# Where a graph-attention kernel gets its neighbour channels from: all from HBM, or half of them copied on the chip

## The chip, the core and the metric

The kernel runs on one core of a Trainium2 chip. The metric is the device time of one execution in microseconds (us). A core has the engines TensorE (PE in the profile; its weight loads PEld), VectorE (DVE), ScalarE (ACT), GpSimd (POOL) and SyncE (SP), and 16 DMA engines that move data between the memory of the chip (HBM) and the on-chip memory SBUF, or inside SBUF. The compute engines reach SBUF by partition (128 of them), and PSUM holds what TensorE writes.

## The reference

x has 16 images of 256 channels and 64 x 32 positions, fp32. All that is computed of an image:

```python
alpha = bn_relu(einsum('bchw,oc->bohw', x, wa), ...)      # 32 channels
sigma = bn_relu(einsum('bchw,oc->bohw', x, ws), ...)      # 32 channels
att = einsum('bkn,bkm->bnm', alpha, sigma)
att = softmax(where(adj, att, NEG), axis=2)               # adj: the 8 spatial neighbours
h_s = einsum('bnm,bcm->bcn', att, x)
Gc = einsum('bcn,bdn->bcd', x, x)
catt = softmax(where(cadj, Gc, NEG), axis=2)              # cadj: channels c-1 and c+1 alone
h_p = einsum('bcd,bdn->bcn', catt, x)
out = (1 - gama) * x + gama * elu(h_s + h_p)
```

What matters for the change is h_p: channel c of the output gets channel c-1 and channel c+1 of x, each times a weight of its own.

## The kernel before

**Tiles.** Partition p holds the channels 2p (h = 0) and 2p + 1 (h = 1). Three buffers xs hold images of x, 128 x 2 x 2048 elements with a row of zeros ahead and behind. `upper` (two buffers) holds x once more, by position instead of by channel, in halves of 1024 and 1152 KB. An image is worked on in four quarters of 512 positions (QUARTERS, QN = 512), so there are 64 steps; step s is quarter s mod 4 of image s // 4.

**The neighbour channels.** For h = 0 the neighbours of channel 2p are 2p + 1, which is in the same partition of xs, and 2p - 1, which is in partition p - 1. For h = 1 they are 2p, in the same partition, and 2p + 2, in partition p + 1. The neighbour in the same partition is handled by ACT (`weigh_own`, L301), which writes weight times x (plus 1) into PSUM tile z. The other neighbour lies in another partition, where an engine can't reach it, and so the host lays out a third copy of x (`x_near`) in which it stands in the right partition: h = 0 gets channel 2p - 1, h = 1 gets channel 2p + 2, zeros at the ends. It is loaded into `near` (two buffers) one quarter at a time, 128 x 2 x 512 elements, 512 KB (`load_near`, L173). `mix_channels` on DVE (L383) multiplies it by its weight and adds it to z. Then TensorE adds the spatial part to z (`z_sums`), from `upper` and the transposed probabilities.

**The rest of a step.** TensorE computes the scores, DVE masks them and takes maxima, ACT the exponentials, DVE normalises, TensorE transposes, ACT moves the result to SBUF, TensorE runs the two phases of `z_sums`, ACT and DVE take the ELU (`exp_z`, `elu_out`), and POOL scales and adds x (`keep_x` L237, `add_elu` L243 and L247) into `blend`, which SP stores. Once an image TensorE projects x of the next image onto queries and keys (`project_odd` in the step of quarter 0, `project_query`, `project_even`) and computes the products of neighbouring channels from `upper` (`gram_band`, in the step of quarter 3), from which DVE and ACT make the channel weights catt.

**Order.** Each engine runs a list of instructions written out in the order of the steps t, with waits on semaphores. All big DMAs are issued by SP, on one queue. In step t = 4b + q, SP waits for the scores and transposes, loads a quarter of near of image b + 1, waits for the first phase of z_sums of the step before (`z_half`), loads a half of x of image b + 2 (q = 0 and 2), the second half of upper of image b + 1 (q = 1) or the first half of upper of image b + 2 (q = 3), and stores the result of step t - 2. A half of upper is loaded only once `z_done` tells that the image two before has been used up; so the second half, issued in the step of q = 1, is wanted by `gram_band` two steps later. Ahead of the loop stand the loads of the first images: x(0), upper(0), the constants, then, behind a wait for `project_odd(0)`, the first quarter of near(0) and both halves of x(1), and behind the first scores the other three quarters of near(0).

Of the kernel before, what the change touches and what calls it, by code (L numbers as in the profile page):

```python
# [6 lines left out]
B, C, H, W = 16, 256, 64, 32  # L7
HID = C // 8
P = 128
HALF = C // P  # L10
N = H * W
QUARTERS = P // HID
QR = H // QUARTERS
QN = QR * W
# [5 lines left out]
XBUFS = 3  # L20
# [6 lines left out]
SIDES, PAIRS, POWERS = 100, 104, 108  # L27
EVEN, ODD = 5 * KEYS, 4 * KEYS
HALVES = N // 2


C_ID, C_DOWN = 0, P
# [8 lines left out]
def graph_attention(nc, x, x_t, x_near, w_t, vectors, constants, out):  # L41
# [15 lines left out]
    with ctx:  # L57
        def sb(name, shape, dt=fp32):
            return ctx.enter_context(nc.sbuf_tensor(name, shape, dt))
# [4 lines left out]
        def sem(name):  # L64
            return ctx.enter_context(nc.semaphore(name))

        xs = [sb(f"x{j}", [P, HALF, N + 4 * W]) for j in range(XBUFS)]
        near = [sb(f"near{j}", [P, QUARTERS, HALF, QN]) for j in range(2)]
        upper = [sb(f"upper{j}", [P, GROUPS + 1, C]) for j in range(2)]
        const = sb("const", [P, C_ALL])  # L70
        zeros_b = sb("zeros_b", [P, QN], bf16)
# [18 lines left out]
        catt = sb("catt", [P, 2, 2])  # L90
# [15 lines left out]
        masks_in = sem("masks_in")  # L106
        ident_in = sem("ident_in")
        x_in = [[sem(f"x_in{j}{i}") for i in range(2)] for j in range(XBUFS)]
        near_in = [[sem(f"near_in{j}{q}") for q in range(QUARTERS)] for j in range(2)]
        upper_in = [[sem(f"upper_in{j}{i}") for i in range(2)] for j in range(2)]  # L110
        stored = [sem(f"stored{i}") for i in range(BLENDS)]
        pads_done = sem("pads_done")
        zeros_done = sem("zeros_done")
        bn_step = sem("bn_step")
        bn_var = sem("bn_var")
# [24 lines left out]
        mix_done = sem("mix_done")  # L140
# [12 lines left out]
        def real(s):  # L153
            return 0 <= s < STEPS

        def cols(q):
            return slice(W + q * QN, W + (q + 1) * QN)

        @block.sync
        def _(sp):  # L160
            def load_x(b, i):
                if b >= XBUFS:
                    s = (b - XBUFS) * QUARTERS + 2 * i + 1
                    sp.wait_ge(even_done, b - XBUFS + 1)
                    sp.wait_ge(product_done, 2 * s + 2)
                    sp.wait_ge(keep_done, s + 1)
                sp.dma_start(xs[b % XBUFS][:, :, W + i * HALVES:W + (i + 1) * HALVES],
                             x_img[b][:, :, i * HALVES:(i + 1) * HALVES]).then_inc(x_in[b % XBUFS][i], 16)

            def load_near(b, q):  # L170
                if b >= 2:
                    sp.wait_ge(mix_done, 2 * ((b - 2) * QUARTERS + q) + 2)
                sp.dma_start(near[b % 2][:, q, :, :], x_near[b, q]).then_inc(near_in[b % 2][q], 16)  # L173

            def load_by_key(b, i):
                if b >= 2:
                    sp.wait_ge(z_done, (b - 2) * QUARTERS + 2 * i + 2)
                part = slice(i * GROUPS // 2, (i + 1) * GROUPS // 2 + i)
                sp.dma_start(upper[b % 2][:, part, :], x_t[b][:, part, :]).then_inc(upper_in[b % 2][i], 16)

            def store(s):
                b, q = s // QUARTERS, s % QUARTERS
                if s < TAIL:
                    sp.wait_ge(blend_done, s + 1)
                    sp.dma_start(out_img[b, :, :, q * QN:(q + 1) * QN], blend[s % BLENDS][:, :, :])\
                        .then_inc(stored[s % BLENDS], 16)
                else:
                    for h in range(HALF):
                        sp.wait_ge(tail_done, 2 * (s - TAIL) + h + 1)
                        sp.dma_start(out_img[b, :, h, q * QN:(q + 1) * QN], blend[s % BLENDS][:, h, :])\  # L190
                            .then_inc(stored[s % BLENDS], 16)

            sp.dma_start(const[:, 0:C_BAND], constants[:, 0:C_BAND]).then_inc(ident_in, 16)
            load_x(0, 0)
            load_x(0, 1)
            load_by_key(0, 0)
            load_by_key(0, 1)
            sp.dma_start(const[:, C_BAND:], constants[:, C_BAND:]).then_inc(masks_in, 16)
            sp.wait_ge(odd_done, 1)
            load_near(0, 0)  # L200
            load_x(1, 0)
            load_x(1, 1)
            sp.wait_ge(score_done, 2)
            for q in range(1, QUARTERS):
                load_near(0, q)
            load_by_key(1, 0)
            for t in range(STEPS + 2):
                b, q = t // QUARTERS, t % QUARTERS
                if real(t):
                    sp.wait_ge(score_done, t - t % 2 + 2)  # L210
                    if t > 0:
                        sp.wait_ge(pt_done, t)
                if b + 1 < B:
                    load_near(b + 1, q)
                if t > 0 and real(t):
                    sp.wait_ge(z_half, t)
                if q % 2 == 0 and b + 2 < B:
                    load_x(b + 2, q // 2)
                if q == 1 and b + 1 < B:
                    load_by_key(b + 1, 1)  # L220
                if q == 3 and b + 2 < B:
                    load_by_key(b + 2, 0)
                if real(t - 2):
                    store(t - 2)
            for i in range(BLENDS):
                sp.wait_ge(stored[i], 16 * (STEPS // BLENDS + (i >= TAIL % BLENDS)))

        @block.gpsimd
        def _(pool):
            def keep_x(s):  # L230
                b, q = s // QUARTERS, s % QUARTERS
                if s == 0:
                    pool.wait_ge(bn_var, 1)
                pool.wait_ge(x_in[b % XBUFS][q // 2], 16 * (b // XBUFS + 1))
                if s >= BLENDS:
                    pool.wait_ge(stored[s % BLENDS], 16 * (s // BLENDS))
                nc.gpsimd.tensor_scalar(blend[s % BLENDS][:, :, :], xs[b % XBUFS][:, :, cols(q)], mix[:, 0:1],  # L237
                                        0.0 if s < TAIL else mix[:, 1:2],
                                        ALU.mult, ALU.add).then_inc(keep_done, 1)

            def add_elu(s):
                pool.wait_ge(elu_done, 2 * s + 2)
                nc.gpsimd.tensor_scalar(elu[s % 2][:, :, :], elu[s % 2][:, :, :], vec[:, V_GAMA:V_GAMA + 1], mix[:, 1:2],  # L243
                                        ALU.mult, ALU.add).then_inc(gama_done, 1)
                pool.wait_ge(keep_done, s + 1)
                pool.wait_ge(gama_done, s + 1)
                nc.gpsimd.tensor_tensor(blend[s % BLENDS][:, :, :], elu[s % 2][:, :, :], blend[s % BLENDS][:, :, :],  # L247
                                        ALU.add).then_inc(blend_done, 1)

            for j in range(XBUFS):  # L250
                nc.gpsimd.memset(xs[j][:, :, 0:W], 0.0).then_inc(pads_done, 1)
                nc.gpsimd.memset(xs[j][:, :, W + N:N + 2 * W], 0.0).then_inc(pads_done, 1)
            pool.wait_ge(bn_done, 1)
            for t in range(STEPS + 2):
                if real(t - 1):
                    keep_x(t - 1)
                if 0 <= t - 2 < TAIL:
                    add_elu(t - 2)
# [84 lines left out]
        def _(dve):  # L343
# [33 lines left out]

            def mix_channels(s, h):
                b, q = s // QUARTERS, s % QUARTERS
                dve.wait_ge(near_in[b % 2][q], 16 * (b // 2 + 1))  # L380
                dve.wait_ge(product_done, 2 * s + h + 1)
                zh = z[s % 2][h]
                nc.vector.scalar_tensor_tensor(zh[:, :], near[b % 2][:, q, h, :], catt[:, h, h:h + 1],  # L383
                                               zh[:, :], ALU.mult, ALU.add).then_inc(mix_done, 1)

            def elu_out(s, h):
# [40 lines left out]
            part = vec[:, 0:8].rearrange("p (s n) -> p n s", s=2)  # L427
# [15 lines left out]
            for t in range(STEPS + 2):  # L443
                b, q = t // QUARTERS, t % QUARTERS
# [215 lines left out]
```

## Time and profile before

| | |
|---|---|
| Median of 3 runs (lowest, highest) | 419.72 us (418.23, 424.91) |
| The profiled execution | 416.75 us, span 415.0 us |
| Mean granted clock of TensorE | 0.964 of full speed |
| PE busy | 364.1 us, 88% of the span |
| PEld busy | 277.5 us, 67% |
| DVE busy | 315.5 us, 76% |
| ACT busy | 305.8 us, 74% |
| POOL busy | 291.6 us, 70% |
| DMA | 137.74 MB in 40613 packets, mean 332 GB/s |
| The chain that ended last, by engine | PE 32%, DMA 30%, DVE 20%, ACT 9%, issue 7% |
| Issues: x | 32 of 1024 KB, 9.1 us from issue to landing |
| Issues: near | 64 of 512 KB, 7.8 us |
| Issues: upper | 16 of 1152 KB, 8.4 us, and 16 of 1024 KB, 7.9 us |
| Issues: stores | 62 of 512 KB, 8.0 us, and 4 of 256 KB, 2.1 us |

The profiled execution is one run of the program with the profiler on; its time of 416.75 us is the span of the core's work and 1.75 us around it. Busy is the sum of the times in which an engine ran an instruction. The chain follows what released what, back from the last instruction. "Issue" is time in which nothing that the profile shows was waited for. The time to landing is from the issue of a DMA by SP until its semaphore is full, so it holds the time that it stood in the queue behind others.

### The profile page before, as it was taken

The page shows a single profiled execution, that of the slowest core. Times are in us where ns is not written, and L with a number is a line of the kernel's source. Part 1 is how long each engine was busy: PE and PEld are TensorE (multiplying, and loading weights), DVE is VectorE, ACT ScalarE, POOL GpSimd, SP SyncE. Part 2 cuts the span into 40 slices and gives each one's busy share as a digit, 9 for nine tenths or more (in the row PEclk, how much of TensorE's full clock was granted, in tenths as well). Part 3 has the DMA queues.
Part 4 walks back from the last instruction along what each step waited for, and adds up shares of the span by engine and source line. Part 5 has one row for each costly group of instructions (what it writes and reads, how often), then busy time and mean ns, then how long its engine had stood idle before and what let it go on. Part 6 is the DMA issues. An engine that isn't in the chain of part 4 may idle for free.

```text
span 415.0 us, 14346 instructions
## 1 busy us (share of the span) xinstructions
PE 364.1 (88%) x5487; PEld 277.5 (67%) x5488; DVE 315.5 (76%) x1072; ACT 305.8 (74%) x900; POOL 291.6 (70%) x198
## 2 busy tenths in 40 slices
PE   5977998989998999999899999999989898999783
PEld 1546767666766867676686767677676667767662
DVE  1166978778787688879768887978788697888775
ACT  2178686868878497887849788787869678686761
POOL 2007686787868588787858878788868858787861
PEclk9889999999999899999989999999999899999778
DMA  8999999999999899999999999999999999985213
GB/s 274 414 368 404 315 344 357 366 359 347 364 346 385 292 358 366 388 364 351 356 317 337 382 385 360 363 378 383 342 367 358 365 307 367 341 297 202 103 53 152
DMA packets 40613, 137.74 MB, mean 332 GB/s; under 512 B 3296, under 2 KB 3552, under 8 KB 36448
## 3 DMA queue, kind: packets, MB, share of 16 engines
q1 hardware_dynamic: 40256, 136.76, 91.4%
q8 instruction: 43, 0.70, 0.6%
q14 instruction: 26, 0.21, 0.1%
q10 hardware_dynamic: 288, 0.07, 0.1%
HBM read 103.26 MB, written 33.55 MB: 330 GB/s over the span
## 4 chain that ended last, share of the span: by engine, by line
PE 32%; DMA 30%; DVE 20%; ACT 9%; issue 7%; SPq 0%; DVEq 0%; ACTq 0%
DMA upper<-x_t_dram 28%; PE gb L468 17%; PE z L468 11%; ACT score L281 6%; DVE probs L374 5%; DVE elu L389 5%; PE tr L543 3%; DVE z L383 3%; ACT z L301 3%; DMA x<-x_dram 2%; DVE gb L404 1%; DVE band L400 1%; DVE row_inv L370 1%; DVE pair_inv L420 1%; DVE catt L421 1%
## 5 line engine op out<-in xcount | busy, mean ns | idle before, releaser
L468 PEld LDWEIGHTS z<-probs_t,upper 64*128 64x128 f32 x2304 | 155.6, 191 | 44.6 <-issue 28.8
L468 PE MATMUL z<-probs_t,upper 64*128 64x128 f32 (+1 forms) x2304 | 173.5, 284 | 5.1 <-ACT probs_t L292 2.4
L247 POOL TENSOR_TENSOR blend<-elu,blend 128x1024 f32<-128x1024 f32 x62 | 146.2, 2358 | 9.5 <-POOL elu L243 0.4
L243 POOL TENSOR_SCALAR elu<-elu,vec,mix 128x1024 f32<-128x1024 f32 x62 | 74.0, 1193 | 98.5 <-DVE elu L389 98.5
L308 ACT ACTIVATE elu<-z 128x512 f32<-128x512 f32 x128 | 69.6, 597 | 60.6 <-PE z L468 60.6
L389 DVE SCALAR_TENSOR_TENSOR elu<-elu,z 128x512 f32<-128x512 f32 x124 | 79.5, 683 | 28.7 <-ACT elu L308 28.3
L301 ACT ACTIVATE z<-x,catt 128x512 f32<-128x512 f32 x128 | 83.6, 693 | 14.2 <-DVE catt L421 14.1
L281 ACT ACTIVATE score<-score,neg_max 128x128 f32<-128x128 f32 x256 | 86.2, 337 | 7.4 <-DVE neg_max L365 7.3
L383 DVE SCALAR_TENSOR_TENSOR z<-near,catt,z 128x512 f32<-128x512 f32 x128 | 90.3, 751 | 1.5 <-ACT z L301 1.5
L237 POOL TENSOR_SCALAR blend<-x,mix 128x1024 f32<-128x1024 f32 x64 | 72.0, 1126 | 6.5 <-DMA x<-x_dram 6.5
L468 PE MATMUL gb<-x,wt 128*32 128x256 f32 (+2 forms) x720 | 65.1, 480 | 2.5 <-DMA x<-x_dram 2.5
L365 DVE CUSTOM_DVE_ANT_0 score<-score,const 128x128 f32<-128x128 f32 x256 | 66.4, 322 | 1.1 <-PE score L468 1.1
L543 PE MATMUL tr<-const,probs 128*128 128x128 f32 x256 | 42.9, 291 | 17.0 <-DVE probs L374 16.4
L468 PE MATMUL gb<-upper 128*64 128x65 f32 (+1 forms) x1088 | 41.5, 237 | 14.9 <-DMA upper<-x_t_dram 14.8
L281 ACT ACTIVATION_READ_ACCUMULATOR score<-score,neg_max 128x1 f32 x256 | 51.9, 203 | 0.0
L468 PEld LDWEIGHTS gb<-upper 128*64 128x64 f32 (+1 forms) x1088 | 38.4, 149 | 19.8 <-issue 18.5
L374 DVE TENSOR_TENSOR probs<-score,row_inv 128x512 f32<-128x512 f32 x64 | 44.3, 692 | 2.4 <-DVE row_inv L370 0.3
L543 PEld LDWEIGHTS tr<-const,probs 128*128 128x128 f32 x256 | 27.4, 143 | 24.5 <-DVE probs L374 23.2
L292 ACT ACTIVATE probs_t<-tr 128x512 f32<-128x512 f32 x64 | 38.4, 600 | 5.8 <-PE tr L543 5.7
L468 PE MATMUL score<-key,query 32*64 32x128 f32 x1024 | 36.5, 279 | 0.0
L365 DVE DVE_READ_ACCUMULATOR2_ANT neg_max<- 128x1 f32 x256 | 36.3, 142 | 0.0
L468 PEld LDWEIGHTS gb<-x,wt 128*32 128x32 f32 x720 | 19.0, 110 | 23.6 <-issue 14.9
(49 smaller groups left out, 145.0 us busy)
## 6 DMA issues: line engine op xcount, KB each, us to landing
x<-x_dram SPq DMA_DIRECT2D x32, 1024.0 KB, 9.1
near<-x_near_dram SPq DMA_DIRECT2D x64, 512.0 KB, 7.8
out_dram<-blend SPq DMA_DIRECT2D x62, 512.0 KB, 8.0
upper<-x_t_dram SPq DMA_DIRECT2D x16, 1152.0 KB, 8.4
upper<-x_t_dram SPq DMA_DIRECT2D x16, 1024.0 KB, 7.9
out_dram<-blend SPq DMA_DIRECT2D x4, 256.0 KB, 2.1
const<-constants_dram SPq DMA_DIRECT2D x1, 291.5 KB, 12.0
const<-constants_dram SPq DMA_DIRECT2D x1, 128.0 KB, 2.2
```

Of the source, the lines that this page charges most:

```text
L237: nc.gpsimd.tensor_scalar(blend[s % BLENDS][:, :, :], xs[b % XBUFS][:, :, cols(q)], mix[:, 0:1], 0.0 if s < TAIL else mix[:, 1:2], ALU.mul ...
L243: nc.gpsimd.tensor_scalar(elu[s % 2][:, :, :], elu[s % 2][:, :, :], vec[:, V_GAMA:V_GAMA + 1], mix[:, 1:2], ALU.mult, ALU.add).then_inc(ga ...
L247: nc.gpsimd.tensor_tensor(blend[s % BLENDS][:, :, :], elu[s % 2][:, :, :], blend[s % BLENDS][:, :, :], ALU.add).then_inc(blend_done, 1)
L281: last = nc.scalar.activation(at, at, ACT.Exp, bias=neg_max[s % 2][:, v:v + 1], scale=-1.0, accum_out=row_sum[s % 2][:, v:v + 1])
L301: nc.scalar.activation(z[s % 2][h][:, :], xs[b % XBUFS][:, 1 - h, cols(q)], ACT.Identity, scale=catt[:, h, 1 - h:2 - h], bias=1.0).then_in ...
L308: nc.scalar.activation(elu[s % 2][:, h, :], z[s % 2][h][:, :], ACT.Exp, bias=-1.0)\
L365: last = nc.vector.tensor_tensor_reduce(at, at, mask, -1.0, TOP, ALU.add, ALU.min, neg_max[s % 2][:, v:v + 1])
L374: nc.vector.tensor_tensor(probs[s % 2][:, :, :], score[s % 2][:, :].rearrange("p (v m) -> p v m", m=WIN), row_inv[s % 2][:, :].unsqueeze(2 ...
L383: nc.vector.scalar_tensor_tensor(zh[:, :], near[b % 2][:, q, h, :], catt[:, h, h:h + 1], zh[:, :], ALU.mult, ALU.add).then_inc(mix_done, 1)
L389: nc.vector.scalar_tensor_tensor(to, elu[s % 2][:, h, :], 1.0, z[s % 2][h][:, :], ALU.min, ALU.max).then_inc(elu_done, 1)
L468: return nc.tensor.matmul(o, l, r, start=start, stop=stop, skip_group_check=True, **kw)
L543: last = nc.tensor.transpose(tr[:, v * P:(v + 1) * P], probs[s % 2][:, v, :], ident)
```

## The change

The h = 1 half of near, channel 2p + 2, is channel 2(p + 1), which is the h = 0 row of partition p + 1 of xs. It no longer comes from HBM: DMAs copy it inside SBUF from partitions 1 to 127 of xs into partitions 0 to 126 of near, in two pieces, 112 partitions and then 15. The h = 0 half still comes from HBM. near is loaded by halves of an image (1024 positions) instead of quarters: a DMA of 512 KB from HBM, a copy of 448 KB and one of 60 KB, whose three increments of 16 are awaited together (NEARS). Partition 127 of near's h = 1 half has no neighbour and must be zero; POOL sets both buffers of near to zero once, at the start. load_near has a wait more, for the half of x that it copies from, and at first for the zeros; load_x has a wait more, since a buffer of x may be overwritten only once it has been copied from. The steps in which near is loaded are now those of q = 0 and 2. The layout of x_near on the host shrinks to the h = 0 rows.

```diff
+SPREAD = 112
+NEARS = 3 * 16
...
-        near = [sb(f"near{j}", [P, QUARTERS, HALF, QN]) for j in range(2)]
+        near = [sb(f"near{j}", [P, HALF, N]) for j in range(2)]
...
-        near_in = [[sem(f"near_in{j}{q}") for q in range(QUARTERS)] for j in range(2)]
+        near_in = [[sem(f"near_in{j}{i}") for i in range(2)] for j in range(2)]
...
             def load_x(b, i):
...
+                    sp.wait_ge(near_in[(b - XBUFS) % 2][i], NEARS * ((b - XBUFS) // 2 + 1))
...
-            def load_near(b, q):
+            def load_near(b, i):
+                sp.wait_ge(x_in[b % XBUFS][i], 16 * (b // XBUFS + 1))
+                if b < 2:
+                    sp.wait_ge(near_zero, b + 1)
                 if b >= 2:
-                    sp.wait_ge(mix_done, 2 * ((b - 2) * QUARTERS + q) + 2)
-                sp.dma_start(near[b % 2][:, q, :, :], x_near[b, q]).then_inc(near_in[b % 2][q], 16)
+                    sp.wait_ge(mix_done, 2 * ((b - 2) * QUARTERS + 2 * i + 1) + 2)
+                j, signal, xb = b % 2, near_in[b % 2][i], xs[b % XBUFS]
+                part = slice(i * HALVES, (i + 1) * HALVES)
+                from_x = slice(W + i * HALVES, W + (i + 1) * HALVES)
+                sp.dma_start(near[j][:, 0, part], x_near[b][:, part]).then_inc(signal, 16)
+                for lo, hi in ((0, SPREAD), (SPREAD, P - 1)):
+                    sp.dma_start(near[j][lo:hi, 1, part], xb[lo + 1:hi + 1, 0, from_x]).then_inc(signal, 16)
...
             sp.wait_ge(score_done, 2)
-            for q in range(1, QUARTERS):
-                load_near(0, q)
+            load_near(0, 1)
             load_by_key(1, 0)
...
-                if b + 1 < B:
-                    load_near(b + 1, q)
+                if q % 2 == 0 and b + 1 < B:
+                    load_near(b + 1, q // 2)
...
                 nc.gpsimd.memset(xs[j][:, :, W + N:N + 2 * W], 0.0).then_inc(pads_done, 1)
+            for j in range(2):
+                nc.gpsimd.memset(near[j][:, :, :], 0.0).then_inc(near_zero, 1)
...
             def mix_channels(s, h):
                 b, q = s // QUARTERS, s % QUARTERS
-                dve.wait_ge(near_in[b % 2][q], 16 * (b // 2 + 1))
+                dve.wait_ge(near_in[b % 2][q // 2], NEARS * (b // 2 + 1))
                 dve.wait_ge(product_done, 2 * s + h + 1)
                 zh = z[s % 2][h]
-                nc.vector.scalar_tensor_tensor(zh[:, :], near[b % 2][:, q, h, :], catt[:, h, h:h + 1],
+                nc.vector.scalar_tensor_tensor(zh[:, :], near[b % 2][:, h, q * QN:(q + 1) * QN], catt[:, h, h:h + 1],
                                                zh[:, :], ALU.mult, ALU.add).then_inc(mix_done, 1)
```

## Rows read from the trace of the kernel before

**Rows 1.** The page: the span in 40 slices, the busiest DMA queue, and HBM traffic.

```profile
DMA  8999999999999899999999999999999999985213
GB/s 274 414 368 404 315 344 357 366 359 347 364 346 385 292 358 366 388 364 351 356 317 337 382 385 360 363 378 383 342 367 358 365 307 367 341 297 202 103 53 152
...
q1 hardware_dynamic: 40256, 136.76, 91.4%
...
HBM read 103.26 MB, written 33.55 MB: 330 GB/s over the span
```

**Rows 2.** Windows by stage: busy us of each engine (instructions), TensorE clock, DMA share, GB/s.

```profile
98.00:124.00 26.00, 23.59 (x360) 17.65 (x360) 21.39 (x70) 21.13 (x61) 20.29 (x14) 1.00 1.02 357
124.00:150.00 26.00, 23.23 (x350) 18.06 (x346) 19.86 (x70) 18.95 (x57) 18.75 (x13) 0.93 0.94 338
150.00:176.00 26.00, 24.72 (x386) 18.76 (x380) 22.14 (x77) 21.96 (x67) 21.64 (x14) 1.00 1.02 376
...
358.00:384.00 26.00, 24.20 (x398) 18.91 (x398) 21.97 (x80) 20.69 (x59) 20.06 (x14) 1.00 0.76 264
```

**Rows 3.** Waits of the engines: engine, line, releaser, us in total, times, longest us.

```profile
PE gb L468 <- DMA upper<-x_t_dram: 14.8, 14, 2.2
...
PE gb L468 <- DMA x<-x_dram: 2.5, 1, 2.5
```

**Rows 4.** Chain that ended last, in order of time: start us, us, what.

```profile
29.54 9.60 DMA upper<-x_t_dram
...
102.78 8.23 DMA upper<-x_t_dram
111.14 2.37 PE gb L468 x68
...
126.38 9.08 DMA upper<-x_t_dram
135.60 3.63 PE gb L468 x68
...
366.96 7.97 DMA upper<-x_t_dram
```

**Rows 5.** Windows near the start, where only loads move; columns as in the second group.

```profile
8.00:10.00 2.00, 0.00 (x0) 0.00 (x0) 0.00 (x0) 0.00 (x0) 2.00 (x2) 0.99 1.04 430
10.00:12.00 2.00, 1.81 (x20) 1.03 (x24) 0.00 (x0) 0.00 (x0) 0.00 (x0) 0.50 1.04 442
```

**Rows 6.** Windows at the end, where only stores move; columns as in the second group.

```profile
386.00:390.00 4.00, 2.75 (x27) 2.32 (x28) 3.93 (x13) 3.29 (x12) 3.29 (x4) 0.85 0.36 135
...
406.00:410.00 4.00, 2.65 (x36) 2.37 (x36) 1.97 (x4) 1.20 (x3) 0.62 (x1) 1.00 0.68 262
```

**Rows 7.** Instructions on tile near: count, ns min/median/max, first and last start us.

```profile
L383 DVE SCALAR_TENSOR_TENSOR z<-near,catt,z x128: 748/751/756, 21.8 to 402.9; 128x512 f32<-128x512 f32 x128
L173 SPq DMA_DIRECT2D near<-x_near_dram x64: 327/333/1103, 12.2 to 374.8; - x64
...
DMA to landing us min/median/max: 5.0/7.8/10.4
```

**Rows 8.** Landing of the loads of x: us from issue, min/median/max.

```profile
DMA to landing us min/median/max: 6.4/9.1/11.7
```

**Rows 9.** Timeline of TensorE near the start: start us, us, instruction, idle before it.

```profile
22.99 1.40 PE L468 MATMUL gb<-x,wt 128*32 128x256 f32 x16 [2.51 <-DMA x<-x_dram]
```

**Rows 10.** Timeline of GpSimd near the start, columns as in the group before.

```profile
1.14 0.15 POOL L252 MEMSET x<- 128x64 f32 x1
7.78 2.21 POOL L237 TENSOR_SCALAR blend<-x,mix 128x1024 f32<-128x1024 f32 x2 [6.49 <-DMA x<-x_dram]
32.95 1.19 POOL L243 TENSOR_SCALAR elu<-elu,vec,mix 128x1024 f32<-128x1024 f32 x1 [22.96 <-DVE elu L389]
```

**Rows 11.** Timeline of SP's DMA issues near the start, columns as before.

```profile
12.18 0.33 SPq L173 DMA_DIRECT2D near<-x_near_dram  x1
12.55 1.21 SPq L167 DMA_DIRECT2D x<-x_dram  x2
```

More of the change, by code:

```diff
@@ L112, in graph_attention @@
         pads_done = sem("pads_done")
+        near_zero = sem("near_zero")
         zeros_done = sem("zeros_done")
@@ L645 @@
     keys = keys.reshape(B, P, HALF, GROUPS + 1, WIN).transpose(0, 4, 3, 2, 1).reshape(B, WIN, GROUPS + 1, C)
-    beside = np.pad(a["x"].reshape(B, C, N), ((0, 0), (1, 1), (0, 0)))
-    beside = np.stack([beside[:, 0:C:2], beside[:, 3:C + 2:2]], axis=2)
-    beside = beside.reshape(B, P, HALF, QUARTERS, QN).transpose(0, 3, 1, 2, 4)
+    beside = np.pad(a["x"].reshape(B, C, N), ((0, 0), (1, 1), (0, 0)))[:, 0:C:2]
     arrays = {"x_dram": a["x"], "x_t_dram": keys, "x_near_dram": beside, "w_dram": w_t, "vectors_dram": vectors,
```

## The prediction, made before the change was run

> **What bounds the kernel now.** I read the page first. In its 40 slices the DMA line stands at 9 from the second slice to the thirty-fifth, and one queue, SP's, fills 91.4% of the 16 DMA engines' span with 136.76 MB [rows 1]. Is it really full where the work repeats? The windows say yes: share 0.94 to 1.02 at 338 to 376 GB/s, with TensorE busy 23 to 25 of 26 us, and only behind 358 us does the share fall, to 0.76 [rows 2]. Two resources are nearly full, so I looked for who waits for whom. TensorE waits for the upper tile (x by position) 14 times, 14.8 us in all, about 1 us an image, and once, 2.5 us, for x [rows 3]. The chain in order of time shows the loop: the load of an upper half is issued, lands 8 to 9.6 us later, gram_band starts at once, and 15 us of compute later the next one can be issued. From the piece at 29.54 to that at 366.96 there are 14 images: 24.1 us each [rows 4]. Those 8 us are mostly a place in a full queue: one MiB at the best rate of [rows 5], 430 GB/s, would take 2.4 us. So the DMA engines and TensorE's order are tied, DMA slightly the later: DMA time added to an image shows nearly whole, DMA time taken away shows only up to the 14.8 us of waits.
>
> How full is full? Loads alone ran at 430 and 442 GB/s [rows 5], stores alone at 135/0.36 = 375 and 262/0.68 = 385 GB/s per full share [rows 6]. HBM read is 103.26 MB and written 33.55 [rows 1], per image 6.45 and 2.10 MB. Unmixed that is 6.45/0.430 + 2.10/0.380 = 15.0 + 5.5 = 20.5 us. An image takes 24.1 at a share of about 0.99 [rows 2, 4], so 23.9. The 3.4 us between are lost when traffic out of SBUF mixes with loads: 3.4/2.10 = 1.6 us per MB going out.
>
> **Part by part.** A half image of near needs 1 MiB in both versions. Before, all came from HBM, in two DMAs of 512 KiB (64 in all). Now 512 KiB come from HBM in one DMA, 448 KiB are copied from 112 partitions of x and 60 KiB from 15: 96 issues instead of 64.
>
> Issues: 32 more at 0.33 us [rows 7] are 10.6 us of SP over the whole run, and SP spends its time in waits. I put them at nothing; if SP became late, their price would be 0.66 us an image.
>
> The load half. Same bytes, rows of 4 KB as before, issued up to one step earlier than the odd quarters were. It is read a whole image later, and a near load took at most 10.4 us [rows 7]: nothing. Ahead of the upper half in the queue stands the same number of bytes, issued about a step sooner.
>
> The copies, where all hangs. The trace of before has no transfer inside SBUF. Low end: a copy moves like loads alone, 0.524 MB/0.430 = 1.22 us, where in the steady mix at 357 GB/s [rows 2] a load costs 1.47: a gain of 0.25 us per half image. It could also relieve HBM: 1.04 of an image's 8.55 MB leave it, 12%, and 12% of the 3.4 us is 0.4 an image, 0.2 per half. High end: the 112 partitions at half rate, 0.459/0.215 = 2.13 us, and the 15 at a quarter, 0.061/0.108 = 0.57, together 2.70, a loss of 1.5 over the 1.22. What I take: a copy reads SBUF as a store does and writes it as a load does, so the nearest row is the mixing cost. 0.52 MB x 1.6 = +0.85 us per half, less 0.2 of relief: +0.65. Of the 32 halves the first two lie in the start and the last two where the share is 0.76 or falling; 28 x 0.65 = +18.2 us.
>
> The rows show that an on-chip row must pass the same 16 engines. The Trainium skill (DMA: Bandwidth & Descriptors, "Where 436 GB/s comes from") has it that the HBM side, about 358 GB/s, binds loads and the fabric, 435, binds copies inside SBUF; by that the copies would gain the 0.25 us per half and no more would be lost. This trace speaks against the first half of it: 430 and 442 GB/s of loads [rows 5].
>
> The start. The first half of near is issued at 12.18 us, right ahead of both halves of x(1) [rows 11]. It now carries 0.52 MB more, 1.2 us. TensorE waited 2.51 us for that very x until 22.99 us [rows 9]: +1.2 us on the path. mix_channels first runs at 21.8 us [rows 7], some 9.6 us behind the issue; hidden by about 4 us.
>
> The two memsets of near on GpSimd: 4096 elements a partition. A 64-column memset takes 0.15 us, a 1024-column operation 1.1 [rows 10]; so 4.5 us (by the second) to 9.7 us (64 x 0.152) each. Behind 1.3 us the first ends at 11 us at worst, before the issue at 12.18; the second by 20.7, before SP's first step. Both delay keep_x from 7.78 by up to 13 us, whose result add_elu takes at 32.95 [rows 10]: covered. Were it not, the start would slip by the excess.
>
> New waits on SP. load_near now waits for its half of x, issued one image (24 us) earlier and landed after at most 11.7 us [rows 8]; behind it in SP's order are the wait for z_half, the load of x, the store and the upper half. load_x waits for the near copy of three images back. Both long met: nothing. mix_channels waits for a half where it waited for a quarter: nothing, since near comes an image early.
>
> DVE reads 512 elements in a row as before: 751 ns stay [rows 7]. Less for nobody: no instruction of an engine goes.
>
> Sum: 416.75 (the profiled execution, whose span is 415.0) + 18.2 + 1.2 = 436.2, 4.7% over. The median of the runs is 419.72, 3 us above that execution, so I say 437.
>
> **The rivals.** Copies cost what loads cost. For it: row size and byte count are equal. Each half is 0 to 0.25 us dearer: 416.75 + 1.2 + 0 to 7 = 418 to 425; no difference that a measurement of this kernel can tell, which starts at 2%, 8.4 us.
>
> Relief decides, and the time falls. The mechanism: reads from HBM are what stalls, and with 16% fewer of them the queue drains sooner, so the upper half lands before TensorE asks. 0.25 + 0.2 per half x 28 = 12.6 us, less 1.2: 405. It is capped by the 14.8 us of waits [rows 3], plus what the clock gives back: gram_band took 2.37 us at 111.14 and 3.63 at 135.60, behind a wait [rows 4], and the window around the second has clock 0.93 [rows 2]. Three such windows (the first stands in [rows 2]) at some 2 us: at best 398. It decides once a copy costs less than 1.47 us. Against it: loads alone run at 430.
>
> The copies crowd. Their sixteen rows at a time are not spread as a whole tile's are, and the engines wait on each other in SBUF: the high end, 28 x 1.5 + 1.2 = +43, 460. TensorE then waits 4 us an image for upper, and its clock falls more often. The trace of before can't speak to this. The Trainium skill (SBUF — State Buffer, "Door 1: The DMA port swizzle") says the port of a partition follows from certain bits of its number; by that the last 15 partitions share four ports and the 112 are cut across them, which would give this case.
>
> One ring. If the 60 KiB went through a single engine, at 430/16 = 27 GB/s that is 2.3 us per half on one ring, all others waiting at the semaphores: +64, 482.
>
> **Numbers.** My forecast (0.3 to 1.1 us per half, 426 to 449): 0.40. Crowding, 449 to 465: 0.14. One ring: 0.04. Equal cost: 0.22. Relief: 0.18. A rest of 0.02 for a mishap that I don't see. Slower by over 2% (above 428): 0.58; within: 0.24; faster (below 411): 0.18. The range leaves out the one ring, the top of crowding and the better half of relief: 408 to 465.
>
> **What would show it.** Right: TensorE's wait for upper rises from 1 to 2 or 3 us an image, the image from 24.1 to 25.3 or more, the DMA share stays near 1 while the rate falls from 357 toward 335 GB/s, and HBM read falls to 86.5 MB. Crowding: the rate under 320. Relief: the rate above 365 or the share under 0.95, waits for upper near nothing. Wrong in the start: keep_x or SP's first step late, x(1) more than 2 us later. I am wrong altogether if SP's added waits are ever last to be met.

## The result and the profile after

The changed kernel took 436.61 us (median of 4 runs, 434.87 to 440.93) beside 418.98 us of the kernel before on the same chip: ratio 1.0466, 95% interval 1.0345 to 1.0587. It is slower. Medians here are over all runs of a kernel, while the ratios and their intervals leave out runs in a slower state of the chip, so that a ratio can differ a little from that of the medians. Its profiled execution has a span of 439.1 us where that of before had 415.0: 24.1 us are to be found.

The page of the changed kernel: the DMA share and rate in 40 slices, SP's queue, and HBM traffic.

```profile
DMA  8999899999999999999999999999999989997222
GB/s 248 347 328 324 240 347 310 352 370 362 350 345 318 318 341 352 362 367 273 358 328 321 334 353 364 304 345 347 339 341 349 369 274 346 332 343 245 96 79 115
...
q1 hardware_dynamic: 40704, 136.63, 93.8%
...
HBM read 86.48 MB, written 33.55 MB: 273 GB/s over the span
```

Against [rows 1] the queue carries the same 136.6 MB, and 16.8 MB less of it come from HBM (86.48 instead of 103.26 MB). The DMA line is as full as before and the rates are lower, most of all at the start (slices 3 to 5: 328, 324, 240 GB/s where there were 368, 404, 315).

TensorE's waits for DMA in the changed kernel, columns as in [rows 3]:

```profile
PE gb L481 <- DMA upper<-x_t_dram: 24.5, 12, 5.0
...
PE z L481 <- DMA x<-x_dram: 5.2, 1, 5.2
...
PE gb L481 <- DMA x<-x_dram: 4.2, 1, 4.2
```

The waits for upper went from 14.8 to 24.5 us, with one of 5.0 us; the wait for x(1) from 2.5 to 4.2 us. That is 11.4 of the 24.1 us. The wait for x(0), at the very start, went from 3.7 to 5.2 us; before, its row was:

```profile
PE z L468 <- DMA x<-x_dram: 3.7, 1, 3.7
```

Those 1.5 us fall before any load or copy of near is issued, so they are hardly the copies' doing. TensorE's busy time tells of most of the rest:

```profile
PE 374.3 (85%) x5487; PEld 285.5 (65%) x5488; DVE 319.7 (73%) x1072; ACT 306.9 (70%) x900; POOL 298.1 (68%) x200
```

Before it was 364.1 us for the same instructions: 10.2 us more, at a mean granted clock of 0.928 instead of 0.964. The chain of the changed kernel shows where such time starts (start us, us, what):

```profile
33.82 12.29 DMA upper<-x_t_dram
46.24 4.14 PE gb L481 x68
...
63.79 8.39 DMA upper<-x_t_dram
```

The upper half that was issued at 33.82 us lands after 12.29 us; gram_band then takes 4.14 us instead of 2.37: TensorE had waited 4.97 us, and its granted clock is 0.50 of full speed (1.2 instead of 2.4 GHz) from 46 to 50 us. These loads in the chain are second halves of upper, one an image. In the kernel before, the one after that at 29.54 us [rows 4] stands at 54.51:

```profile
54.51 8.65 DMA upper<-x_t_dram
```

So the second image went by in 25.0 us before and takes 30.0 us now. The last of these loads is issued at 366.96 us before [rows 4]; SP's timeline has it at 389.97 now:

```profile
389.97 0.34 SPq L191 DMA_DIRECT2D upper<-x_t_dram  x1
```

Three stretches, then. Until the first load that the chain shows: 29.54 against 33.82, +4.3 us. The image after it: +5.0 us. The 13 images from there: 312.45 us before (24.03 each), 326.18 now (25.09 each), +13.7 us. Behind that 1.1 us more. The sum is 24.1.

### The profile page after: what moved, and what is told of

It is laid out like the page before. It is cut to its first block, busy times and chain, and to the rows that moved or that the text cites. A ratio compares the mean times of both kernels' runs of the same rounds, so it can differ in the third digit from the quotient of the medians.

```text
span 439.1 us, 14412 instructions
## 1 busy us (share of the span) xinstructions
PE 374.3 (85%) x5487; PEld 285.5 (65%) x5488; DVE 319.7 (73%) x1072; ACT 306.9 (70%) x900; POOL 298.1 (68%) x200
## 3 DMA queue, kind: packets, MB, share of 16 engines
HBM read 86.48 MB, written 33.55 MB: 273 GB/s over the span
## 4 chain that ended last, share of the span: by engine, by line
PE 35%; DMA 30%; DVE 17%; ACT 8%; issue 7%; SPq 1%; DVEq 0%; ACTq 0%
DMA upper<-x_t_dram 26%; PE gb L481 16%; PE z L481 14%; DMA x<-x_dram 5%; ACT score L294 4%; DVE probs L387 4%; DVE elu L402 4%; PE tr L556 3%; ACT z L314 2%; DVE z L396 2%; PE score L481 2%; DVE gb L417 1%; DVE band L413 1%; ACT elu L321 1%; DVE row_inv L383 1%
## 5 line engine op out<-in xcount | busy, mean ns | idle before, releaser
L481 PEld LDWEIGHTS z<-probs_t,upper 64*128 64x128 f32 x2304 | 160.6, 196 | 44.5 <-issue 27.4
L481 PE MATMUL z<-probs_t,upper 64*128 64x128 f32 (+1 forms) x2304 | 178.8, 290 | 4.7 <-ACT probs_t L305 2.1
L481 PE MATMUL gb<-x,wt 128*32 128x256 f32 (+2 forms) x720 | 66.6, 489 | 5.4 <-DMA x<-x_dram 4.2
L481 PE MATMUL gb<-upper 128*64 128x65 f32 (+1 forms) x1088 | 43.8, 244 | 24.5 <-DMA upper<-x_t_dram 24.5
L481 PEld LDWEIGHTS gb<-upper 128*64 128x64 f32 (+1 forms) x1088 | 40.5, 157 | 29.3 <-issue 28.1
L413 DVE TENSOR_TENSOR band<-const,gb 128x195 f32<-128x195 f32 x16 | 5.7, 358 | 43.8 <-PE gb L481 43.7
L481 PEld LDWEIGHTS gb<-x,wt 128*32 128x32 f32 x720 | 19.7, 112 | 26.9 <-issue 18.8
```

The costliest lines, as they stand in the source:

```text
L481: return nc.tensor.matmul(o, l, r, start=start, stop=stop, skip_group_check=True, **kw)
```

## The experiments

Each kernel below starts from the changed one, if nothing else is said, and is timed beside the kernel before. Its median was 418.73 us beside the first four, 418.14 us beside the 15 partitions alone, both pieces not shifted and the first two with three buffers, and 416.27 us beside the other three. The lines that fit NEARS, the number of increments awaited, and the host's x_near to each kernel aren't shown.

**Halves from HBM.** Both neighbour channels come from HBM again, everything else stays.

```diff
-                sp.dma_start(near[j][:, 0, part], x_near[b][:, part]).then_inc(signal, 16)
-                for lo, hi in ((0, SPREAD), (SPREAD, P - 1)):
-                    sp.dma_start(near[j][lo:hi, 1, part], xb[lo + 1:hi + 1, 0, from_x]).then_inc(signal, 16)
+                sp.dma_start(near[j][:, :, part], x_near[b][:, :, part]).then_inc(signal, 16)
```

> The changed kernel with both neighbour channels from HBM again, by halves of an image (one DMA of 1 MiB); waits, memsets and order stay those of the changed kernel. Theories: CROWDING (the copies' rows go to the partitions unevenly, so that DMA engines wait for each other in SBUF), CROSSING (any byte that leaves SBUF and enters it again costs more among loads, however its rows are spread), ORDER (the halves, the new waits and the memsets cost, not the copies). CROWDING and CROSSING both expect the time of the kernel before, ratio 0.99 to 1.01, 415 to 423 us, and 14 to 18 us of TensorE waits for upper. ORDER expects 1.03 to 1.05, 432 to 440 us.

422.65 us, ratio 1.0073 (1.0007 to 1.0138). The halves, the memsets and the new waits cost some 3 us, at the edge of what is measured; ORDER is out as the main cause. In the profiled execution of this kernel TensorE waited 19.9 us for upper, more than the 14 to 18 that I had expected.

**No copies.** The loop with the two copies is taken out, and NEARS is 16.

> The changed kernel without both copies; the h = 1 neighbour channel is left out (zeros are added in its place), all else stays. CROWDING and CROSSING expect a kernel faster than the one before: 16.7 MB less pass the DMA engines, so TensorE's 14.8 us of waits for upper and the clock that they cost go, 398 to 406 us, ratio 0.95 to 0.97. ORDER expects 425 us or more. The difference to the changed kernel is the whole price of the copies, 30 to 38 us by my forecast of 1.22 + 0.65 us per half image less what TensorE can't use.

421.12 us, ratio 0.998 (0.982 to 1.014), runs from 409 to 436 us. CROWDING and CROSSING expected a ratio of 0.95 to 0.97, and the interval leaves that out; a gain of 1% it doesn't. Its profiled execution had a granted clock of 0.817 and isn't compared here. So 16.7 MB less through the DMA engines is worth little at most, which already speaks against the bound that I took them for.

**A whole tile's copy.** As many bytes (512 KB) go from SBUF to SBUF, but in one DMA over all 128 partitions, each onto itself. The h = 1 neighbour is then channel 2p in place of 2p + 2, here and wherever rows aren't shifted below.

```diff
-                for lo, hi in ((0, SPREAD), (SPREAD, P - 1)):
-                    sp.dma_start(near[j][lo:hi, 1, part], xb[lo + 1:hi + 1, 0, from_x]).then_inc(signal, 16)
+                sp.dma_start(near[j][:, 1, part], xb[:, 0, from_x]).then_inc(signal, 16)
```

> The changed kernel with the two shifted copies replaced by one of all 128 partitions onto themselves (512 KB; the h = 1 neighbour is then channel 2p instead of 2p + 2), so the same way through SBUF with a whole tile's spread of rows. CROWDING expects the time of the kernel before or less: ratio 0.97 to 1.01, 406 to 423 us. CROSSING expects the price to stay: 1.03 to 1.05, 432 to 440 us.

417.65 us, ratio 0.998 (0.992 to 1.004). The whole loss is gone. This is the run that decides between CROWDING and CROSSING: a copy inside SBUF costs this kernel no more than the load in its place, if all 128 partitions are in one DMA.

**112 partitions alone.** The copy of 15 is left out.

```diff
-                for lo, hi in ((0, SPREAD), (SPREAD, P - 1)):
-                    sp.dma_start(near[j][lo:hi, 1, part], xb[lo + 1:hi + 1, 0, from_x]).then_inc(signal, 16)
+                sp.dma_start(near[j][0:SPREAD, 1, part], xb[1:SPREAD + 1, 0, from_x]).then_inc(signal, 16)
```

> The changed kernel with the copy of 112 partitions alone; the 15 partitions' neighbour channel is left out (zeros). CROWDING by the last 15 rows, which sit together: most of the loss goes with 12% of the bytes, ratio 0.99 to 1.02. CROWDING by the 112 as well: ratio 1.02 to 1.035, the 15 being worth 0.45 us of the 1.1 us per half that a spread copy would not cost. CROSSING: the loss shrinks by its bytes, 12% of it, ratio 1.035 to 1.045.

430.86 us, ratio 1.031 (1.021 to 1.041): the 112 cost by themselves. This kernel issues as many DMAs as that with the whole tile's copy, and moves less, so it isn't the number of DMAs that costs.

**15 partitions alone.** The same edit with the other piece.

> The changed kernel with the copy of 15 partitions alone; the 112 partitions' neighbour channel is left out (zeros). The 112 alone gave 1.031. If the two pieces crowd each by itself and add up, the 15 rows cost 0.0466 - 0.031 = 0.015 over their absence: ratio 1.005 to 1.02, 421 to 427 us, against 0.998 without any copy. If they cost only where they meet the 112, the time is that without copies, 0.99 to 1.005.

417.77 us (10 runs) beside 418.14 of before, 0.999 by the medians; these runs give no interval. The runs of both kernels spread over more than 10 us, so a cost of up to 1% would not be seen. The changed kernel's 1.047 and the 1.031 of the 112 have intervals that overlap, so whether the 15 cost something beside the 112 stays open.

**Both pieces, not shifted.**

```diff
-                    sp.dma_start(near[j][lo:hi, 1, part], xb[lo + 1:hi + 1, 0, from_x]).then_inc(signal, 16)
+                    sp.dma_start(near[j][lo:hi, 1, part], xb[lo:hi, 0, from_x]).then_inc(signal, 16)
```

> The changed kernel with both copies, 112 and 15 partitions, but each partition copied onto itself instead of from the one above (the h = 1 neighbour is then channel 2p instead of 2p + 2). CROWDING by how the rows are dealt out to the engines expects no change from the changed kernel: ratio 1.035 to 1.055, 433 to 442 us. CROWDING by the shift (a row read at another place than it is written) expects the time of the whole-tile copy: 0.99 to 1.01, 415 to 423 us.

436.98 us, ratio 1.046 (1.039 to 1.053), the changed kernel's own. Reading one partition above the one that is written costs nothing that shows; the cut into 112 and 15 does.

**The cut, from HBM.** The h = 1 channel comes from HBM, in 112 and 16 partitions. It computes all that the reference does.

```diff
-                sp.dma_start(near[j][:, 0, part], x_near[b][:, part]).then_inc(signal, 16)
-                for lo, hi in ((0, SPREAD), (SPREAD, P - 1)):
-                    sp.dma_start(near[j][lo:hi, 1, part], xb[lo + 1:hi + 1, 0, from_x]).then_inc(signal, 16)
+                sp.dma_start(near[j][:, 0, part], x_near[b][:, 0, part]).then_inc(signal, 16)
+                for lo, hi in ((0, SPREAD), (SPREAD, P)):
+                    sp.dma_start(near[j][lo:hi, 1, part], x_near[b][lo:hi, 1, part]).then_inc(signal, 16)
```

> The changed kernel with the h = 1 neighbour channel loaded from HBM, but in two pieces of 112 and 16 partitions, as the copies were cut. CROWDING at the write (rows dealt to the engines so that several write one part of SBUF at a time) expects the loss to stay, whole or for the most part: ratio 1.02 to 1.05, 427 to 440 us. CROWDING at the read alone (the source in SBUF) expects the time of the halves from HBM: 1.00 to 1.015, 419 to 425 us.

440.85 us, ratio 1.059 (1.052 to 1.067). No byte is copied on the chip, and the loss is there in full. So the writes of the cut tile are enough for it.

**64 and 64 partitions.** The unshifted copy with SPREAD = 64 and P in place of P - 1: all partitions, cut in the middle.

> The copy of all partitions onto themselves (the h = 1 neighbour is then channel 2p instead of 2p + 2), cut into 64 and 64 partitions. The Trainium skill (SBUF — State Buffer, Door 1: The DMA port swizzle) has it that 64 neighbouring partitions reach half of the ports. If that is what crowds, the two pieces lose at least as much as 112 and 15: ratio 1.04 to 1.09, 435 to 457 us. If the loss came from the uneven counts of 7 rows and 1 row to an engine, two even pieces of 4 rows cost nothing: 0.99 to 1.01, 415 to 423 us.

439.52 us, ratio 1.059 (1.051 to 1.066). Two equal pieces don't help, so uneven counts of rows aren't the cause. That the rows of a shorter DMA lie less well over the 16 engines is what CROWDING says and what is left of the theories; which engine writes which partition no view here shows. The packets tell what the cut does to them. The trace holds the duration of each DMA packet; these are the 4 KB ones (x and near) and the 8 and 9 KB ones (upper), in ns:

```
kernel               4 KB: median  90th of 100   mean | 8 KB mean  9 KB mean
before                     159        159        174  |    417        449
whole tile's copy          159        159        167  |    436        485
changed                    199        309        222  |    360        369
112 alone                  195        306        220  |    354        375
cut, from HBM              201        308        223  |    352        374
64 and 64                  208        319        228  |    359        358
```

In every kernel of the table that cuts the tile, half of the 4 KB packets take 195 ns or more, where nine in ten took 159. They aren't only the cut tile's: in the changed kernel 9403 of 16352 take more than 165 ns (before, 1016 of 16384), and the copies are 4064 of them. So at least 5300 slow packets are rows of x and of near's other half. Over the run the 16 engines spend 226.5 us each on 4 KB packets instead of 178.3 in the changed kernel, and get back 17.6 us on upper.

TensorE's waits for upper follow: halves from HBM, whole tile's copy, then both pieces unshifted, the cut from HBM, and 64 and 64.

```profile
PE gb L479 <- DMA upper<-x_t_dram: 19.9, 14, 2.7
```

```profile
PE gb L480 <- DMA upper<-x_t_dram: 14.3, 12, 2.4
```

```profile
PE gb L481 <- DMA upper<-x_t_dram: 21.2, 13, 3.4
```

```profile
PE gb L481 <- DMA upper<-x_t_dram: 22.0, 12, 3.7
```

```profile
PE gb L481 <- DMA upper<-x_t_dram: 26.2, 14, 4.3
```

They are 14.3 us with the whole tile and 21 to 26 us with the cuts, but 19.9 us with the halves from HBM, where nothing is cut: taken alone, the waits don't tell a cut kernel from a whole one. The time of an image does it better. From the third load of a second half of upper to the last, 13 images on, SP's timelines give 24.03 us an image before, 24.48 with halves from HBM and 23.97 with the whole tile's copy, against 25.09 in the changed kernel, 24.77 with the 112 alone, 25.18 unshifted, 25.11 with the cut from HBM and 25.23 with 64 and 64 (one execution each).

Does the longer queue cost, or the lost rate? A third buffer of upper tells. It lets both halves be issued two steps earlier, on the kernel before and on the changed one:

```diff
+UBUFS = 3
...
-                if q == 1 and b + 1 < B:
-                    load_by_key(b + 1, 1)
-                if q == 3 and b + 2 < B:
-                    load_by_key(b + 2, 0)
+                if q == 1 and b + 2 < B:
+                    load_by_key(b + 2, 0)
+                if q == 3 and b + 2 < B:
+                    load_by_key(b + 2, 1)
```

(upper and its semaphores count by UBUFS, the wait on z_done is for b >= UBUFS, and load_by_key(1, 1) stands ahead of the loop.)

**Three buffers, kernel before.**

> The kernel before with three buffers of upper instead of two, its halves issued two steps earlier (so the load doesn't wait for the image two before, and gram_band finds it landed). LOOP (TensorE's 14.8 us of waits for upper come from the issue being late and a queue of 8 us ahead of it; the DMA engines have room left): the waits go, ratio 0.955 to 0.98, 400 to 410 us. RATE (the DMA engines are full, and the wait only moves to another load): ratio 0.99 to 1.01, and a wait for x or near shows instead.

396.70 us, ratio 0.951 (0.944 to 0.958): 21 us faster than the kernel before, and it computes all that the reference does. TensorE's only waits for DMA in it are these two:

```profile
PE z L470 <- DMA x<-x_dram: 4.7, 1, 4.7
...
PE gb L470 <- DMA x<-x_dram: 1.4, 1, 1.4
```

**Three buffers, changed kernel.**

> The changed kernel with three buffers of upper, issued two steps earlier. LOOP (the crowding costs since it makes the queue ahead of upper longer): the loss goes, ratio 0.97 to 1.00, 405 to 419 us. RATE (the crowding costs since it takes the DMA engines' time, of which nothing is left): the loss stays, ratio 1.03 to 1.05, 431 to 440 us, with the wait moved to x or near.

433.50 us, ratio 1.035 (1.024 to 1.046). RATE holds here. No wait for upper is left, and others have come:

```profile
PE gb L483 <- issue: 21.6, 11, 4.2
...
PE gb L483 <- DMA x<-x_dram: 7.1, 1, 7.1
```

The first of them is put down to "issue", which names no releaser. The time does. TensorE's timeline and SP's have:

```profile
179.76 1.94 PE L483 MATMUL gb<-x,wt 128*32 128x256 f32 x16 [2.90 <-issue]
```

```profile
166.19 0.63 SPq L172 DMA_DIRECT2D x<-x_dram  x1
```

The matmul that waits 2.90 us reads x, whose last half was issued 13.6 us before and landed at 179.67 us by the last update of its semaphore. In all 11 of these waits the matmul starts 0.1 us or less after a half of x has landed. So the wait has moved from upper to x. Beside 396.70 us for the kernel before with three buffers, the cut now costs some 9%.

**Three buffers and the whole tile's copy.** The one edit on top of the other.

> The whole-tile copy of partitions onto themselves (the h = 1 neighbour is then channel 2p instead of 2p + 2) together with three buffers of upper. The kernel before with three buffers gave 0.951. If a well-spread copy costs the DMA engines what a load does, the same: 0.945 to 0.965, 395 to 404 us. If taking 16% of the reads off HBM is worth something once TensorE no longer waits for upper: under 0.945. If a copy costs more than a load and the loop hid it: 0.97 or more.

397.63 us, ratio 0.956 (0.951 to 0.962), against 0.951 (0.944 to 0.958) from HBM alone. A copy in one piece is no better than the load that it stands for, even where TensorE no longer waits for upper.

The windows of 100 to 340 us set the five side by side: before, changed, and with three buffers before, changed, and whole tile's copy (columns as in [rows 2]).

```profile
100.00:340.00 240.00, 220.26 (x3420) 170.40 (x3412) 193.47 (x660) 188.66 (x560) 185.94 (x120) 0.98 1.00 358
```

```profile
100.00:340.00 240.00, 213.87 (x3249) 164.18 (x3248) 186.71 (x634) 181.32 (x534) 176.75 (x115) 0.97 1.02 340
```

```profile
100.00:340.00 240.00, 228.32 (x3644) 176.69 (x3641) 204.42 (x694) 199.74 (x593) 197.03 (x128) 1.00 1.02 378
```

```profile
100.00:340.00 240.00, 217.15 (x3292) 165.17 (x3292) 187.97 (x641) 185.29 (x545) 179.47 (x117) 0.96 1.02 349
```

```profile
100.00:340.00 240.00, 228.40 (x3648) 176.51 (x3642) 204.45 (x695) 200.82 (x597) 196.99 (x128) 1.00 1.02 379
```

The DMA share is 1.00 to 1.02 in all of them, and the rate is 358, 340, 378, 349 and 379 GB/s. A share of 1 doesn't tell that no more can be moved: before, 20 GB/s were still to be had. In the changed kernel 349 is what the third buffer could bring out, below what the kernel before does with two.

## Why the prediction came out right, and where its reasons were wrong

The time (437 for 436.61) and the sign came out, and so did most of what I had said would show it: the rate at 340 GB/s where I looked for 335, 86.5 MB read from HBM; an image is 25.09 us, a little under my 25.3. The waits for upper rose to 24.5 us, about 1.7 an image by the count that gave 1 before, where I looked for 2 or 3. The mechanism behind the case that I had put first did not.

**The bound.** "So the DMA engines and TensorE's order are tied", with DMA "slightly the later". Half right. The loop was: its late issue cost the waits. The rate wasn't full: the same bytes go at 378 GB/s once the third buffer lets them. I took the share of 1.00 for a bound. The asymmetry that I drew from it held all the same for this change, and the cap of 14.8 us on gains did not: the third buffer gave 20.9 us of span (415.0 to 394.1), the waits and 8.9 us of TensorE's busy time (364.1 to 355.2) at a clock of 0.984. With the clock's part I had put the best at 398; that execution took 395.9.

**The price of a copy.** I took +0.85 us per half image for mixing, by the nearest row, less 0.2 for relief. The whole tile's copy measured their sum, and it is nothing: 0.998, to within 0.6%. Copying inside SBUF costs what the load did, and taking 16% of the reads off HBM gains nothing beside it; whether two small effects cancel, this run can't tell. The mixing cost itself was too high: I divided the stores' rate by their share and not the loads', and 430 GB/s at a share of 1.04 is 413, which makes the 3.4 us 2.8. With the third buffer an image takes 22.70 us, 1.3 us less than with two, so at least that much of the 3.4 us wasn't lost by mixing. What costs is the cut of the tile (crowding), which I had as a rival with a chance of 0.14 and with 1.5 us per half. It measured 0.53 us per half in the steady part (1.06 us an image against the kernel before; 0.30 per half against the halves from HBM, 0.56 against the whole tile's copy), a third of that. With three buffers on both sides it is 0.87 us, by twelve images between two issues of upper in SP's timeline. Kernel before with three buffers:

```profile
54.89 0.33 SPq L180 DMA_DIRECT2D upper<-x_t_dram  x1
```

```profile
327.28 0.33 SPq L180 DMA_DIRECT2D upper<-x_t_dram  x1
```

Changed kernel with three buffers:

```profile
63.99 0.34 SPq L192 DMA_DIRECT2D upper<-x_t_dram  x1
```

```profile
357.37 0.34 SPq L192 DMA_DIRECT2D upper<-x_t_dram  x1
```

That is 22.70 and 24.45 us an image. A smaller size put it where my forecast stood; the sign that I had given for crowding, a rate under 320 GB/s, didn't show. The right number came from the wrong step, and by luck.

The Trainium skill has a rule that bears on this. By its SBUF — State Buffer, "Door 1: The DMA port swizzle", 64 neighbouring partitions reach half of the ports. The runs agree in sign: 64 and 64 lose 5.9%. Half the rate for 512 KB would be 1.22 us more per half image, an estimate by that section, and 34 us over 28 halves; the medians differ by 23. By the same section's table the last 15 partitions share four ports, which would make them the worst piece for their size; alone they lost nothing measurable, while the 112 lost 3.1%. So the ports as the cause are not shown.

**The start.** I had +1.2 us. It was 9.3 us up to the third load of a second half of upper: x(1) came 4.4 us later (the matmul that waits for it starts at 27.38 us, not at 22.99 as in [rows 9]; 1.5 of it is the late x(0)), which by my own sign, over 2 us, makes the start wrong, and the next image met a queue of 12.29 us and a wait of 4.97. The issue of that third load in SP's timeline, with halves from HBM and with the whole tile's copy:

```profile
54.89 0.33 SPq L189 DMA_DIRECT2D upper<-x_t_dram  x1
```

```profile
54.48 0.33 SPq L190 DMA_DIRECT2D upper<-x_t_dram  x1
```

Before it was 54.51 us. So the bytes ahead of x(1), which I counted, cost nothing that lasts, and the loss stays only with the cut, which I left out here. My 28 halves at 0.65 were 18.2 us; the 26 from there are 13.7.

**The small terms.** GpSimd's memsets and SP's issues, with the landing of near behind them, in the changed kernel:

```profile
L185 SPq DMA_DIRECT2D near<-x x64: 552/891/1132, 14.0 to 394.6; - x64
L183 SPq DMA_DIRECT2D near<-x_near_dram x32: 328/334/1067, 13.7 to 393.3; - x32
L265 POOL MEMSET near<- x2: 3512/3524/3536, 1.2 to 4.7; 128x4096 f32 x2
...
DMA to landing us min/median/max: 5.5/8.2/12.4
```

A memset takes 3.52 us, below my two bounds, and is hidden. A copy's issue takes more than the 0.33 us of [rows 7]: by their median 0.59 us over 112 partitions and 0.90 over 15. All issues of near together are 61.0 us of SP's time instead of 26.9, so 34 us are added where I had 10.6. It is still hidden, since SP waits far longer for the first phase of z_sums (z_half) alone:

```profile
SPq L227 <- PE z L481: 150.6, 34, 10.6
```

Of the waits added to SP, the one for x shows once, 4.2 us at the start, and SP then waits 4.6 us more for TensorE. So none is last to be met, as I had said.

mix_channels had no wait for near in either kernel, as expected. The halves, memsets and waits together are the 0.7% of the halves from HBM; I had put them at nothing.

**One ring** is out: it wanted 64 us, and the 15 partitions alone cost nothing that shows. **Relief** as the 12.6 us that I priced is out by the whole tile's copy, and by the 16.7 MB left out without such a gain.

## What to carry to other kernels

Keep a tile of 128 partitions in one DMA. A cut into 112 and 15 or 16, or into 64 and 64, cost 4.6 to 5.9% of this kernel at equal bytes, from HBM as well as inside SBUF, and slowed the rows of other loads too; moving reads off HBM gave nothing to set against it. A DMA share near 1 doesn't prove that no more can be moved: before bytes are saved, look in the chain for a load that is issued late for want of a buffer, and give it one.

## What the runs showed of the hardware that I had not expected

The engine that waits pays twice. 9.7 us more of waits for upper and 1.7 for x came with 10.2 us more of TensorE's busy time at a lower granted clock; gram_band took 4.14 us instead of 2.37 right behind a wait of 4.97 us, at a granted clock of 0.50.

What a DMA's issue takes of SP differs by its shape and not by its bytes: 0.33 us for near's h = 0 rows from HBM and 0.33 for a half of upper, 0.61 for a half of x, and inside SBUF 0.81 us over 128 partitions, 0.59 over 112 and 0.90 over 15 (medians; 512, 1024 or 1152, 1024, 512, 448 and 60 KB).

Packets of upper stall by very different amounts: the mean of an 8 KB packet fell from 417 to 360 ns with the cut, rose to 436 with the whole tile's copy, and fell to 371 with the third buffer on the kernel before, where no other load is slowed. What stalls them is open; fewer reads from HBM did not cure it.
